# Two graph products of a GNN kernel: adj as moving operand in runs of 256 columns instead of 512, and their stationary operands placed 64 bytes further

## What is computed

```python
def layernorm(x): return (x - mean(x)) / sqrt(var(x) + 1e-5)     # over the features
h  = x @ W0 + b0
x1 = layernorm(x + (A @ h) / A.sum(-1, keepdims=True))
t  = relu(A @ (x1 @ W1) + b1)
t  = relu(A @ (t  @ W2) + b2)
out = layernorm(x1 + A @ (t @ W3) + b3)
```

## Time and profile before

| | |
|---|---|
| median of three runs | 545.03 us (544.5 to 545.28) |
| profiled execution | 545.27 us |
| its span, first to last instruction | 543.5 us |
| mean granted TensorE clock | 0.995 |
| TensorE matmuls busy | 531.6 us, 3829 instructions |
| VectorE, ScalarE, GpSimd busy | 352.3, 311.2, 212.4 us |
| matmuls of 512 columns in p2 and p5 (744) | 290.0 us busy, summed over the six groups |

### The profile page before, as it was taken

How to read it: one execution, slowest core, us unless ns; L and a number is a source line. 1 busy time by engine, 2 the same in 40 slices (tenths; PEclk the granted TensorE clock), 3 DMA queues, 4 the chain that set the end, 5 groups by cost and what they waited for, 6 DMA issues and landing times.

```text
span 543.5 us, 11026 instructions
## 1 busy us (share of the span) xinstructions
PE 531.6 (98%) x3829; PEld 498.5 (92%) x3829; DVE 352.3 (65%) x1058; ACT 311.2 (57%) x786; POOL 212.4 (39%) x228
## 2 busy tenths in 40 slices
PE   7799999999999999999999999999999999999996
PEld 7788999989899998999989899898999989899896
DVE  4864675757667475675757667475674757657546
ACT  4556655566554756655566555756656566564542
POOL 2865408062270814509063270814509063271100
PEclk9899999999999999999999999999999999999999
DMA  7640070612507033070512507033070511500002
GB/s 267 216 156 1 13 261 1 226 47 62 210 0 270 0 128 142 0 270 0 202 68 58 212 0 270 1 119 151 0 270 0 191 80 54 220 0 40 2 1 77
DMA packets 15286, 58.23 MB, mean 107 GB/s; under 512 B 1952, under 2 KB 2720, under 8 KB 13472
## 3 DMA queue, kind: packets, MB, share of 16 engines
q1 hardware_dynamic: 15264, 57.94, 29.4%
HBM read 49.55 MB, written 8.39 MB: 107 GB/s over the span
## 4 chain that ended last, share of the span: by engine, by line
PE 94%; DVE 2%; DMA 2%; ACT 1%; POOL 1%; SPq 1%; issue 0%; DVEq 0%
PE bank_a L180 16%; PE bank_a L181 16%; PE bank_a L182 16%; PE bank_b L180 15%; PE bank_b L182 15%; PE bank_b L181 15%; DMA y<-in_xT 2%; PE bank_b L273 1%; PE bank_b L274 1%; POOL adj_lo L903 0%; DVE xT_lo L679 0%; DVE stats L790 0%; ACT std L598 0%; DVE moments L802 0%; DVE rstd L787 0%
## 5 line engine op out<-in xcount | busy, mean ns | idle before, releaser
L903 POOL TENSOR_TENSOR adj_lo<-adj_raw,adj_hi 128x512 fp32r<-128x512 f32 x56 | 70.9, 1297 | 263.7 <-ACT adj_hi L489 263.7
L679 DVE TENSOR_TENSOR x_lo<-bank_a,x_hi 128x512 fp32r<-128x512 f32 x62 | 42.9, 692 | 67.3 <-ACT bank_a L579 67.3
L180 PE MATMUL bank_b<-h_hi,adj_hi 128*128 128x256 f32 (+1 forms) x256 | 71.0, 277 | 2.3 <-DVE h_lo L679 2.1
L554 ACT ACTIVATE std<-moments,eps_col 128x1 f32<-128x1 f32 x64 | 18.9, 295 | 92.7 <-DVE moments L760 92.7
L181 PE MATMUL bank_b<-h_lo,adj_hi 128*128 128x256 f32 (+1 forms) x256 | 70.7, 276 | 0.0
L182 PE MATMUL bank_b<-h_hi,adj_lo 128*128 128x256 f32 (+1 forms) x256 | 70.7, 276 | 0.0
L182 PE MATMUL bank_b<-s_hi,adj_lo 128*128 128x256 f32 x232 | 64.1, 276 | 0.0
L180 PE MATMUL bank_b<-s_hi,adj_hi 128*128 128x256 f32 x232 | 64.0, 276 | 0.0
L181 PE MATMUL bank_b<-s_lo,adj_hi 128*128 128x256 f32 x232 | 64.0, 276 | 0.0
L577 ACT ACTIVATE x_hi<-bank_a,b_col 128x512 fp32r<-128x512 f32 x62 | 42.4, 684 | 21.0 <-PE bank_a L182 20.1
L885 POOL TENSOR_TENSOR x1b<-x,b_all 128x256 f32<-128x256 f32 x64 | 45.8, 746 | 17.2 <-DVE x L747 17.2
(11 more groups left out here) (145 smaller groups left out, 1726.7 us busy)
## 6 DMA issues: line engine op xcount, KB each, us to landing
adj_raw<-in_adjT SPq DMA_DIRECT2D x30, 512.0 KB, 5.4
adj_rows<-in_adj SPq DMA_DIRECT2D x14, 1024.0 KB, 9.4
x_raw<-in_x SPq DMA_DIRECT2D x15, 512.0 KB, 7.4
out_y<-y SPq DMA_DIRECT2D x15, 512.0 KB, 2.9
xT_raw<-in_xT SPq DMA_DIRECT2D x14, 512.0 KB, 6.4
w_raw<-in_w SPq DMA_DIRECT2D x4, 256.0 KB, 10.8
adj_rows<-in_adjT SPq DMA_DIRECT2D x2, 512.0 KB, 10.3
xT_raw<-in_xT SPq DMA_DIRECT2D x2, 256.0 KB, 3.3
```

The lines of the kernel that those rows point to most:

```text
L180: pe.matmul(acc, st[0], mv[0], start=start, stop=False)
L554: act.activation(std1[:, j:j + 1], moments1[:, j, 1:2], ACT.Sqrt, bias=eps_col[:, :]).then_inc(std1_ready, 1)
L679: return dve.tensor_tensor(lo, full, hi.bitcast(F32), ALU.subtract)
L903: pool.tensor_tensor(adj_lo[:, s, k, :], raw[:, k, :], adj_hi[:, s, k, :].bitcast(F32), ALU.subtract).then_inc(adj_split, 1)
```

## The change

`adj_product_T` gets a loop over two `side`s of 256 columns around its loop over k, so that each (f, k) has six matmuls of 256 columns in place of three of 512, with the same weights loaded once for each side: 48 matmuls and 48 weight loads a product instead of 24 and 24. The waits for the split tiles stay at the first pass over k (f = 0, first side). And the two small buffers are declared ahead of x1 and s2, so that these two pairs lie 64 bytes further on against adj, while xT and what follows stay where they are.

```diff
         adj_hi, adj_lo = pair("adj", [P, RING, T, N])
+        inv_rows = sb("inv_rows", [P, T], F32)
+        std1 = sb("std1", [P, T], F32)
         x1_hi, x1_lo = pair("x1", [P, T, F])
         s2_hi, s2_lo = pair("s2", [P, T, F])
-        inv_rows = sb("inv_rows", [P, T], F32)
-        std1 = sb("std1", [P, T], F32)
...
-                    for k in range(T):
-                        if f == 0:
-                            pe.wait_ge(split, at(batch, T, k + 1))
-                        mm = three_passes(pe, banks[f][:, :], (st[0][:, k, cols], st[1][:, k, cols]),
-                                          (adj_hi[:, s, k, :], adj_lo[:, s, k, :]), k == 0, k == T - 1)
+                    for side in (slice(0, N // 2), slice(N // 2, N)):
+                        for k in range(T):
+                            if f == 0 and side.start == 0:
+                                pe.wait_ge(split, at(batch, T, k + 1))
+                            mm = three_passes(pe, banks[f][:, side], (st[0][:, k, cols], st[1][:, k, cols]),
+                                              (adj_hi[:, s, k, side], adj_lo[:, s, k, side]), k == 0, k == T - 1)
                     mm.then_inc(done, 1)
```

## The result

The changed kernel takes 557.25 us (median of 6 runs, 555.84 to 559.32) against 545.15 us (6 runs, 544.5 to 545.5) for the kernel before, a ratio of 1.0227 with a 95% interval of 1.0211 to 1.0242. It is slower, by 12.1 us, and so by nearly twice the 6.4 us that the forecast had. Its profiled execution took 556.60 us with a span of 554.7 us, 11.2 us more than the span before.

A forecast was written before the change was run, and what follows sets the result against it. TensorE's own matmul pace was taken to bound the kernel. Split +6.7, edges -0.3, last p5 +0.1 and -0.1 sum to +6.4 us, giving 551.4 us on the median of runs; range 544.4 to 552.4 us.

The forecast's parts named there:

- What bounds the kernel: Whole kernel: TensorE's own matmul pace sets the time, with no waits inside the loop; matmuls busy 531.6 of 543.5 us.
- A second pace: 256-column matmuls, stationary phase 64, moving phase 0: 113.3 or 117.8 ns each, depending on how the stream is entered.
- Matmuls split: p5 and p2: 744 matmuls of 512 columns become 1488 of 256, at the slow pace; +6.7 us.
- own range: Whole kernel, both products slow: 549.5 to 552.4 us, chance 0.50.
- Edges of the 512s: Start of p5: slower first distances, 0.02 us in some 15 steps, go with the 512s; -0.3 us.
- Weight loads and supply of instructions: p5 and p2: 744 more loads, each beside a matmul, and instruction supply cost 0; 0 to +1 us left for supply.
- Earlier deadlines: p2 and p5: split tiles needed sooner, none late in the step; only p5(LAST) tight, +0.1 us.
- Placement alone: p2_first keeps its 512s with x1 in phase 64: 0 to +0.2 us, taken as 0.
- No change: p5 and p2 take the fast pace, leaving only the edge terms; 544.7 us, chance 0.32.
- A fixed part for each matmul: p5 and p2: each of 744 more matmuls costs 3.3 ns, 2.5 us in all; 547.5 us, chance 0.04.
- One product only: Only one of p5 and p2 is slow, half of 6.7 us; 548.1 us, chance 0.12.
- The placement isn't what it says: x1 and s2 stay in phase 0, 256s run on (0, 0); 544.7 to 551.4 us, no chance of its own.

The follow-up runs named there:

- before_p0_plain: Kernel before, with p0 opening without its 512-column matmul and without the join of the two halves; 551.51 us, ratio 1.0116.
- p5 alone: Kernel before, with only s2 moved 64 bytes further on and only p5 split into runs of 256 columns; 548.75 us, ratio 1.0060.
- p2_alone: Kernel before, with only x1 moved 64 bytes further on and only p2 split into runs of 256 columns; 548.14 us, ratio 1.0055.
- open_wide: Changed kernel, with the first pass of each p5 as one matmul of 512 columns; 552.33 us, ratio 1.0135.
- after_padded: Changed kernel, with one p6 matmul in each step split into two of 128 columns, p6's 512 kept; 572.32 us, ratio 1.0507.
- after_p6_plain: Changed kernel, with p6 opening without its matmul of 512 columns; 575.30 us, ratio 1.0563.
- place_only: Kernel before, with only the declarations moved, so x1 and s2 lie 64 bytes further on; 549.49 us, ratio 1.0083.
- phase32: Changed kernel, with inv_rows ahead of x1 and std1 behind s2, putting x1 and s2 at 32 modulo 128; 552.80 us, ratio 1.0138.
- open_wide_p6_plain: Changed kernel, with p5's first pass as one 512-column matmul and p6 opening without its own 512; 545.86 us, ratio 1.0014.
- split_only: Kernel before, with only the loop over sides, p2 and p5 in 256s, x1 and s2 unmoved; 560.84 us, ratio 1.0290.

## Why the prediction was right and wrong

**What bounds the kernel.** Right. TensorE's pace is the time; no wait of the loop appeared.

**A second pace.** Right, and the experiments bear it: p5 and p2 have 281 ns, 11.31 us from the first p5 to the first p6, which is the number written down for the case (96 x 117.8 ns). Whether a stream is fast or slow hangs on its entry; with one wide matmul in p5 both are fast. The evidence was p4(LAST) against p4 of the loop, one product of the tail. before_p0_plain shows the same switch in the open.

Two things in it were too narrow. It tied the two paces to (64, 0), but p3 and p7, on (0, 64), take the slow one as well (p6, p3 and p7 take 11.31 us together in the table above, 117.8 ns for each 256 columns), and so does p1 in before_p0_plain. And it took the phases and the width for all that counts at an entry. The starts in all 13 profiles, sorted by the pace of the last dozen matmuls ahead (near 113 or near 118 ns), show what was missing. A step from (0, 64) to (64, 0) that opens in 256s came out slow behind a fast stretch in all 73 cases that no stall disturbs; behind a slow stretch it came out fast in 19 of 21. That is why p5 was fast in the first step, and it is what sets p6_last, with its slow stretch ahead, apart from p4(LAST). The forecast wrote that slow stretch down and drew nothing from it. Its p5 was right because p1 ran fast.

**Matmuls split.** The term was 6.7 us for p5 and p2, and p5 alone and p2 alone measured 3.5 and 3.0. The term is right. The step that failed is that the sum has no term for what stands behind p2: it puts p6, p3 and p7 at nothing and gives no row for it. Among the signs it reads "p3, p7, p0, p4 and p1 of the step should keep 276 ns". I took L273 for what brings the fast pace at any entry, since p0 and p6 both open with it and both were fast. But p6's L273 had only ever been seen behind 512s on (0, 0), which come to the fast pace by themselves. Behind the new p2 it left p6, p3 and p7 slow: 95 matmuls x 4.5 ns = 0.43 us a step, the missing 5.5 to 6 us (the table above has 0.41 us a step). I had the paces, the number of matmuls and the list of products behind; what wasn't asked is where the slow state ends, and from what rows it is known that it ends there. The own range allowed for "a few products that escape" and not for products that are drawn in, and so 557 us lay outside it. The 6.7 us themselves were no luck: where only p5 or only p2 was split, the sum without a term for the products behind came out.

**Edges of the 512s.** -0.3 us is not shown. The changed kernel has only one fast p5, that of the first step, with 5.45 us, and the same step's p5 took 5.44 us before. In open_wide, where p5 is fast from the second step on, it takes 5.44 to 5.45 us against 5.46 to 5.47, some 0.02 us, but there it opens with a 512.

**Weight loads and supply of instructions.** No stall came, so 0 was right for this kernel. The doubt beside it, "a stall at each of the few turns of the loop would be some tenths of a us each", had no row for its size and missed it: with three pairs more in the loop body each of three jumps costs 4.7 us and 3 us of half clock, 15.1 us in all in after_padded and 18.1 us in after_p6_plain against the changed kernel.

**Earlier deadlines.** Right: no wait on x1 or s2 in the loop. p5(LAST) took 5.59 us where it took 5.61; the rows don't separate its small terms from its pace.

**Placement alone.** I took 0 to +0.2 us for p2_first and said nothing of what 512s on (64, 0) would do in p2 and p5, since these were to be split. place_only shows it: 5.60 us instead of 5.44 for such a product, 4.2 us in all. The "some 9 ns over 226.7" that the forecast reads off L273 is a slip, since 0.24 us is 13 ns over; in place_only each such matmul costs 6.6 ns more.

**The rivals.** "No change" is out: the matmuls ran at a pace that depends on the places of their operands and on what ran before. The page "SBUF — State Buffer" of the Trainium skill, section "Who interferes with whom", gives the moving operand and the weight load two independent ports; 545, 549, 553, 557 and 561 us for the same arithmetic from the same buffers at other offsets and widths speak against taking that to mean that placement is free. "A fixed part for each matmul" is out: with p5's wide opening and the plain p6, the split costs 0.6 us where 2.5 were named, and its slow first step alone takes 0.85 us longer than the first step before (33.51 against 32.66 us). The forecast quotes for this rival, from the Trainium skill's page "TensorE: Matmul & The Clock Gate", section "Back-to-back issue gap", a formula that the page gives for a matmul by itself; for a stream of weight loads and matmuls it gives about 131 ns at 512 columns. This trace agrees with neither: it has 226.7 ns. "One product only" exists, as an experiment. "The placement isn't what it says" is out in so far as the declarations alone moved the time (549.49 us), and with the split 32 and 64 bytes differ (552.80 and 557.25 us); the addresses themselves stand in no trace.

**What stays open.** What TensorE hands from one product to the next. It has at least three values. A fast p2 in 256s was followed, through L273, by a slow p6 each time (the first step of the changed kernel, 14 steps of open_wide, the last p2 of p2_alone); but p2 at 281 ns was followed by a slow p6 in the changed kernel and by a fast one in p2_alone, in phase32 and in the first step of open_wide. A gap of a tenth of a us can switch the pace too: in the last p2 of p2_alone two starts come 150 and 220 ns after the ones before, and the slow stretch goes on at the fast pace; in the third step of open_wide_p6_plain p1 begins with 180 and 230 ns behind a fast p4 and is slow. Only the effects were measured; a conflict between the reads of weight load and moving operand would fit that phases and widths matter, but no run shows it. No version here beats the kernel before: the best, open_wide_p6_plain, stands at 1.0014 (1.0004 to 1.0024).

## What to carry to other kernels

When TensorE bounds a kernel and waits for nothing, look at the mean duration of each group of equal matmuls: 276 and 281 ns for one shape are two paces (113.3 and 117.8 ns from start to start), and 4% of the time of such matmuls lies between them. A slow stretch belongs to the whole chain of products behind it, so before pricing one, find the row that shows where it ends, and check that the entry there will still be the one of the row. A slow stretch ahead is no bad sign by itself: what counts is the pair of paces at the switch, and an entry seen once says little until the pace ahead of it is written down too. A wider matmul at the head of a product can set the pace of the next hundred, for better (p0, and p5 from the second step on) or worse (p6 behind fast 256s, p5 in the first step); and before unrolling or splitting in a long hardware loop, look at the waits named "issue" and at the packets of the instruction queue.

## What the runs showed of the hardware

- fp32r matmuls of 256 columns, back to back with their weight loads at the full clock, start every 113.3, 117.8, 118.3 (phase32: 5.68 us for the 48 of a p5) or 120 ns (split_only: 5.76 us); those of 512 every 226.7 or 233.3 ns (place_only: 5.60 us for 24). The paces hold for dozens of matmuls and end at switches of operands or width, or at a gap.
- The pace of a stretch depends on what ran before it: the same instructions on the same addresses ran p5 and p2 at 276 ns in the changed kernel's first step and at 281 in the others.
- Between two products in 256s of which the first has its stationary operand in phase 0 and its moving one in phase 64, and the second the reverse, a fast stretch was followed by a slow one in 73 of 73 cases and a slow one by a fast one in 19 of 21. Between p6 and p3, p3 and p7, p0 and p4, p4 and p1 of the steps the pace stayed, but for one p1 behind a gap (open_wide_p6_plain).
- Three pairs of weight load and matmul more in TensorE's loop body took the instruction packets from 16 to 43, and left TensorE idle for 4.7 us at each turn, followed by some 3 us at the 1.2 GHz level.
